# Expert numbers loaded into registers ahead of the expert loop of a routed FFN

## The reference, cut to what matters

```python
x = x + attn_a(layernorm(x))
x = x + ffn(layernorm(x), ...)
x = x + attn_b(layernorm(x))
x = x + ffn(layernorm(x), ...)

def ffn(x, ...):              # 8 experts, F = 512
    x = x + attention_16_heads(layernorm(x) * g1 + b1)
    hn2 = layernorm(x) * g2 + b2
    idx = argmax(hn2 @ gate_w + gate_b)              # one expert per token
    mid = relu(hn2 @ w1[e] + b1[e])                  # 128 -> 512
    y   = mid @ w2[e] + b2[e]                        # 512 -> 128, only y[idx[t], t] is kept
    return x + y[idx]
```

## Time and profile before

| | us |
|---|---|
| median of 3 runs | 826.72 |
| lowest, highest | 823.09, 838.03 |
| the profiled execution, its own time | 825.56 |
| its span, first to last instruction | 823.8 |

### The profile page before, as it was taken

The page is one execution under the profiler, slowest core; times in us unless marked ns, Lnnn a source line. Parts: engine busy times, 40 slices in busy tenths (PEclk is TensorE's granted clock), DMA queues, the critical chain, the costliest instruction groups (busy, mean ns, idle before and its releaser), DMA issues.

```text
span 823.8 us, 15612 instructions
## 1 busy us (share of the span) xinstructions
PE 638.2 (77%) x5547; PEld 431.1 (52%) x5549; DVE 508.7 (62%) x1219; ACT 374.0 (45%) x776; POOL 182.8 (22%) x288
## 2 busy tenths in 40 slices
PE   4876799999946777376899999784999899837763
PEld 2654245555445767263566667451445455627663
DVE  7573677767575434685776677264667777464344
ACT  2555066656711333164455555460556667503321
POOL 5206400000004664113000000038000000026552
PEclk8999599999975898696999999886899999958987
DMA  3164752331010111208634320017634220101114
GB/s 81 25 208 113 181 143 60 76 74 28 2 51 23 43 45 30 62 10 194 175 86 86 66 60 4 2 52 171 166 77 89 60 60 3 52 12 43 40 36 122
DMA packets 54836, 59.99 MB, mean 73 GB/s; under 512 B 10376, under 2 KB 47144, under 8 KB 51304
## 3 DMA queue, kind: packets, MB, share of 16 engines
q1 hardware_dynamic: 50952, 52.56, 26.2%
q0 software_dynamic: 2944, 6.04, 2.9%
q10 hardware_dynamic: 864, 0.39, 0.2%
HBM read 39.83 MB, written 18.74 MB: 71 GB/s over the span
## 4 chain that ended last, share of the span: by engine, by line
PE 51%; DVE 17%; DMA 14%; issue 7%; ACT 6%; another core or an unknown queue 2%; SPq 1%; POOL 1%; DVEq 0%; ACTq 0%; POOLq 0%; PEldq 0%
DMA QS<-MT 10%; PE bank L438 9%; PE bank L482 7%; PE bank L454 7%; PE bank L868 5%; PE bank L877 5%; DVE MN L618 3%; DMA KS<-k_parts 2%; DVE HAT L266 2%; PE bank L466 1%; PE bank L511 1%; DVE ST L221 1%; PE bank L458 1%; PE bank L441 1%
## 5 line engine op out<-in xcount | busy, mean ns | idle before, releaser
L618 DVE TENSOR_REDUCE MN<-bank 128x2 f32<-128x512 f32 x384 | 257.8, 690 | 129.5 <-PE bank L438 84.8
L562 ACT ACTIVATE PR<-bank 128x512 f32<-128x512 f32 (+1 forms) x384 | 211.8, 564 | 160.5 <-PE bank L454 98.1
L438 PE MATMUL bank<-KS,QS 126*128 126x256 bf16 (+1 forms) x768 | 157.6, 280 | 23.2 <-DMA KS<-k_parts 16.9
L454 PE MATMUL bank<-QS,KS 128*128 128x256 bf16 (+1 forms) x768 | 147.3, 266 | 21.7 <-DMA QS<-MT 20.4
L482 PE MATMUL bank<-PR,VP 128*32 128x256 f32 (+1 forms) x1536 | 116.1, 376 | 0.7 <-ACT PR L562 0.7
L438 PEld LDWEIGHTS bank<-KS,QS 126*128 126x128 bf16 x768 | 66.0, 104 | 89.1 <-issue 41.2
L702 POOL COPY VP<-V 128x64 f32<-128x64 f32 x96 | 22.1, 236 | 359.6 <-PE bank L482 359.6
L454 PEld LDWEIGHTS bank<-QS,KS 128*128 128x128 bf16 x768 | 72.1, 98 | 44.3 <-DMA QS<-MT 25.1
L877 PE MATMUL bank<-W,PR 128*128 x368 | 58.3, 309 | 29.2 <-ACT PR L894 26.9
L877 PEld LDWEIGHTS bank<-W,PR 128*128 128x128 f32 x368 | 51.9, 218 | 32.6 <-issue 32.6
L1006 DVE TENSOR_TENSOR PR<-bank,B1C 128x512 f32<-128x512 f32 x46 | 31.7, 690 | 59.9 <-PE bank L868 43.5
(11 more groups left out here) (224 smaller groups left out, 880.9 us busy)
## 6 DMA issues: line engine op xcount, KB each, us to landing
QS<-q_parts SPq DMA_DIRECT2D x72, 192.0 KB
KS<-k_parts SPq DMA_DIRECT2D x72, 192.0 KB
k_parts<-KP SPq DMA_DIRECT2D x12, 384.0 KB, 5.5
q_parts<-QP SPq DMA_DIRECT2D x24, 192.0 KB, 5.8
q_parts<-QP SPq DMA_DIRECT2D x24, 128.0 KB, 5.4
W<-in_w SPq DMA_DIRECT2D x1, 2048.0 KB, 13.2
hat_rows<-HAT SPq DMA_DIRECT2D x8, 256.0 KB, 3.0
XT<-moe_out SPq DMA_DIRECT2D x8, 256.0 KB, 3.6
```

What stands on the lines that cost most here:

```text
L438: last = pe.matmul(d, QS[0:SHIFT, bass.ds(slot_of(b) + n * S + qt * P, P)], KS[0:SHIFT, bass.ds(slot_of(b) + n * S, w)], start=True, stop= ...
L454: last = pe.matmul(d, KS[:, bass.ds(slot_of(b) + n * S + kt * P, P)], QS[:, bass.ds(slot_of(b) + n * S + lo, S - lo)], start=True, stop=no ...
L562: act.activation(PR[:, (n % 8) * CH:(n % 8) * CH + w], bank[2 + n % 2][:, 0:w], ACT.Exp, scale=HEAD_SCALE).then_inc(s["exped"], 1)
L618: dve.tensor_reduce(out=o, in_=bank[n % 2][:, :].rearrange("p (t k) -> p t k", k=S), axis=AX_X, op=ALU.max, negate=True).then_inc(s["maxed ...
```

## The change

The four operations that make `EXI` move up between the operations of the slot chain, without waits of their own (the operations that stand between are waited for). PE waits for `experts` right behind the two prefix matmuls and loads all 23 numbers there, ahead of its 16 slot matmuls. DVE loads three numbers behind each of the four SLOT1 operations (12), and the other 11 behind the first two weight copies. Neither loads inside the loop.

```diff
@@ ffn_post_pe
             pe.matmul(bank[5][:, P:2 * P], ONB[:, :], HOTB[:, :], start=True, stop=True).then_inc(s["prefix"], 1)
+            pe.wait_ge(s["experts"], 1)
+            expert = [expert_reg(pe, i) for i in range(NR)]
             pe.wait_ge(s["tile1"], 1)
...
             last.then_inc(s["sums"], 1)
-            pe.wait_ge(s["experts"], 1)
...
-                    e = expert_reg(pe, i)
                     pe.wait_ge(s["relu"], i + 1)
...
-                                         W2[:, bass.ds(e * F + c * P, P)], start=(c == 0), stop=(c == FC - 1))
+                                         W2[:, bass.ds(expert[i] * F + c * P, P)], start=(c == 0), stop=(c == FC - 1))
@@ ffn_post_dve
             ends = a_
+            cmp_i = CMP[:, :].rearrange("p (i e) -> p i e", e=E)
+            dve.tensor_tensor(cmp_i, ends[:, :].rearrange("p (o e) -> p o e", o=1).to_broadcast([P, NR, E]),
+                              I24[:, :].rearrange("p (i o) -> p i o", o=1).to_broadcast([P, NR, E]), ALU.is_le)
             dve_then(dve, dve.tensor_tensor(RT_["base"][:, :], ends[:, :], RT_["n"][:, :], ALU.subtract))
+            dve.tensor_reduce(out=EXF[:, :], in_=cmp_i, axis=AX_X, op=ALU.add)
             dve_then(dve, dve.tensor_scalar(RT_["base"][:, :], RT_["base"][:, :], float(P), None, ALU.mult))
 
+            dve.tensor_scalar(EXF[:, :], EXF[:, :], float(E - 1), None, ALU.min)
             dve_then(dve, dve.tensor_tensor(sl, src, cnt, ALU.subtract))
+            dve.tensor_copy(EXI[:, :], EXF[:, :]).then_inc(s["experts"], 1)
             dve_then(dve, dve.tensor_tensor(sl, te(bank[5][:, 0:P]), sl, ALU.add))
...
+            dve.wait_ge(s["experts"], 1)
+            expert = []
             for c in range(NC):
                 dve.tensor_tensor(SLOT1[:, c * CH:(c + 1) * CH].rearrange("p (t s) -> p t s", s=P),
...
                                   ALU.is_equal).then_inc(s["slot1"], 1)
-
-            cmp_i = CMP[:, :].rearrange("p (i e) -> p i e", e=E)
-            dve_then(dve, dve.tensor_tensor(cmp_i, ends[:, :].rearrange("p (o e) -> p o e", o=1).to_broadcast([P, NR, E]),
-                                            I24[:, :].rearrange("p (i o) -> p i o", o=1).to_broadcast([P, NR, E]),
-                                            ALU.is_le))
-            dve_then(dve, dve.tensor_reduce(out=EXF[:, :], in_=cmp_i, axis=AX_X, op=ALU.add))
-            dve_then(dve, dve.tensor_scalar(EXF[:, :], EXF[:, :], float(E - 1), None, ALU.min))
-            dve.tensor_copy(EXI[:, :], EXF[:, :]).then_inc(s["experts"], 1)
+                expert += [expert_reg(dve, i) for i in range(3 * c, 3 * c + 3)]
...
-            dve.wait_ge(s["experts"], 1)
...
-            expert = [expert_reg(dve, i) for i in range(2)]
...
             first_weights(0)
             first_weights(1)
+            expert += [expert_reg(dve, i) for i in range(3 * NC, NR)]
...
-                    expert.append(expert_reg(dve, i))
                     first_weights(i)
```

## The result

| | before | after |
|---|---|---|
| median of 4 runs, us | 824.9 | 843.34 |
| lowest, highest | 820.76, 838.03 | 843.13, 844.15 |
| profiled execution, own time | 825.56 | 844.15 |
| its span | 823.8 | 842.4 |

The ratio of after to before is 1.0248, with a 95% interval of 1.0207 to 1.0289: slower, by 18 us on the medians and 18.6 on the two profiled spans. The forecast was 848 us, slower.

A forecast was written before the change was run, and what follows sets the result against it. PE held 51% of the chain that ended last, but the edit touched the routing chain, where delaying SUMS delays the layer. 825.56 + 2 x 10.2 + 2.3 + 0.4 - 0.5 = 848.2 us; 8-in-10 range 830 to 858.

The forecast's parts named there:

- The price of a load: Time one register load in a row takes from an engine's sequencer: 0.63 us on DVE, 0.64 on PE.
- The bounds of 0.30 and 0.90: Limits in us for one load: 0.30 if only the load itself counted, 0.90 if each cost what the first did.
- cheap and cold loads: Rivals: loads in a row at 0.30 us each, 830 us total, chance 0.11; at 0.90 us each, 866 us, chance 0.06.
- Part 1: Routing chain: four expert-list operations moved up add 0.7 us to the slot chain; by itself +0.2 us per layer.
- Part 2: Routing chain: PE's 23 loads ahead of its 16 matmuls make SUMS start later, +10.2 us per layer.
- cover and slope: PE's front loads: 3.3 us of DVE work hides their start; each load takes 0.64 us.
- Part 3: DVE's twelve loads between the SLOT1 operations: hidden behind PE's loads; +4.9 us per layer if PE's cover were gone.
- Part 4: DVE's eleven loads after the first two weight copies delay the first bias add: +2.3 us first layer, +0.4 last.
- Part 5: Expert loops without loads: 0.5 us gained in total, bounds nothing and 7 us.
- Both loops again 67 to 71 us: Sign of a right forecast: each expert loop's length from the first L1006 to the last slot's addition.
- The case on the other side: Rival: loads in the expert loops cause the halts; removing them gives back 22 us, total 826 us, chance 0.09.

## Why the prediction was right, point by point

- **The price of a load** (0.63 us on DVE, 0.64 on PE): 0.62 (a third of the 1.87 us from one SLOT1 operation to the next) to 0.65, and 0.645. The bounds of 0.30 and 0.90 are out, and cheap and cold loads with them. The load's own record, 0.301 us, is less than half of the price; the register operation, the assertion and the gaps are the rest.
- **Part 1** (+0.7 us in the slot chain, +0.2 at SUMS): +0.2 with only the list moved. The 184-element comparison lets the next operation through after 0.26 us, the 23-element copy after 0.09, as the timeline of after shows.
- **Part 2** (+10.2 us per layer): +10.3 and +10.0 in the change, +10.3 and +10.1 with PE's front loads alone. The two halves of the working, cover and slope, were measured apart with twelve loads.
- **Part 3** (hidden; 4.9 us uncovered): hidden in the change; 4.3 and 4.0 uncovered. The sequencer starts loading while operations are still queued, which the working left out.
- **Part 4** (+2.3 and +0.4): +1.6 and +0.1. The same omission: the first of the eleven loads starts at 268.5 in the kernel after, ahead of the last small operation of attention b and of both weight copies, and I had it behind them. Beside the kernel with PE's front loads alone, where PE is ready sooner (10.19), DVE's loads do cost 2.3 us in the first layer.
- **Part 5** (-0.5 us, at most -7): not told from nothing; one load in all gives 1.0003, and only the list moved, with all its loads, 1.0026. The 5.3 us of the first loop would have fitted the bound of 7, but the same 5.3 us don't come back where the loops don't vary. "Both loops again 67 to 71 us", a sign of being right, held for the last loop (70.2) and not for the first (63.8).
- The sum of 22.6 us was 4 us above the first pair of traces (18.6). Of these, 1.0 is part 4 and 4.3 the two loops with part 5's 0.5 taken off; some 1.1 us goes the other way, the lateness of the first HOTB. So the total landed at the low end of the forecast's own range (841 to 855), and at the 843.3 from which it called the kernel slower by over 2%: the mechanism was right, and that the verdict held in spite of loops that gave back 4.8 us was partly luck. On the third chip, where the loops don't vary so, the parts add to 22.0 us (HOTB to SUMS +10.3 and +10.0, SUMS to the first bias add +1.7 and 0.0), where parts 1 to 4 said 23.1; on the medians the change cost 21.6 us of 793.
- **The case on the other side**, loads that cause the halts: the kernel before has the same loads and no halts on the third chip, and the kernel after, without loads in its loops, has them on the first. It falls. It was also priced too high: the "as much in the first layer" rested on that loop's length alone, and L1006's waits without a known releaser are 2.6 us there, once, against 13.0 in the last loop.

## What to carry to other kernels

The cost of loading a value into a sequencer's register was here the distance to the engine's next instruction (0.645 us), not the load's record (0.30), and it was a cost only where the engine had nothing queued and was itself waited for. Spread through the loops, 44 loads per layer cost nothing that could be told; gathered ahead of the loop, on the one chain that everything waits for, they were paid in full beyond their cover. Before moving such work early, find the idle time it is to fit in (here 3.3 us for 15 us of loads) and ask what the engine's queue holds behind it.

## What the runs showed of the hardware that was not expected

The same program differs by 4% between the first pair and the later runs, and nearly all of it stands in one kind of stretch. On the first chip both expert loops took 69 us in the kernel before, with halts in which DVE's bias add waited for a releaser that the profile can't name, most of them in the last loop, and they remain in the kernel after, which has no loads in its loops:

```profile
DVE PR L1005 <- remote: 8.6, 3, 4.3
```

Over the whole execution such waits of DVE and ACT sum to 21.4 us before and 19.4 after. In the later traces of both kernels there is none, and their loops took 54 to 55 us with the same instructions; the store-gather pairs went through at 2.58 us each. The halts are not the whole of the 15 us per loop: in the kernel before PE's matmuls were busy for 53.7 and 52.0 us at a granted clock of 0.86 and 0.90 on the first chip, and for 46.6 and 47.0 at 0.99 on the third, so 5 to 7 us of each loop are the same matmuls at a lower clock.

What halts the first chip stays open. That it is the loads in the loops is excluded by the kernel after, which has the halts without them. None of the eight experiments ran there, so nothing else about it was tried.

The sequencers run ahead of their engines: DVE's first front load started at 249.6 in the kernel after, when one operation of TILE1 had just begun (249.54) and another (249.78) and all of SLOT1 (from 250.23) were still to run. So here a load between two operations of an engine cost less than its place in the program says as long as the queue had work, and its full price once it was empty.
